# Fused cross-attention and ternary feed-forward on one core: the places of 22 weight tests, of two statistics and of the first weight transfers are changed

## The reference

```python
x = x + einsum(gelu_tanh(einsum(LN(x), ctx)) * einsum(LN(x), ctx), ctx)   # per batch, 120 context rows
h = silu(tlin(LN(x), w1)) * tlin(LN(x), w2)      # 256 -> 1024
h = gelu(tlin(h, h1))                            # 1024 -> 1024
h = gelu(tlin(h, h2))                            # 1024 -> 1024
x = x + tlin(h, w3)                              # 1024 -> 256
```

## Time and profile before

| what | value |
|---|---|
| median of three executions | 344.42 us (344.0 to 344.77) |
| the profiled execution's own time | 343.81 us |
| its span (first to last instruction) | 341.9 us |
| what lies around the span | 1.9 us |
| mean granted TensorE clock | 0.994 |
| busy: TensorE / VectorE / ScalarE / GpSimd | 325.9 / 265.4 / 219.1 / 47.2 us |
| HBM read, written | 49.36 MB, 6.29 MB |

### The profile page before, as it was taken

How to read it: one execution, slowest core, us unless ns; L and a number is a source line. 1 busy time by engine, 2 the same in 40 slices (tenths; PEclk the granted TensorE clock), 3 DMA queues, 4 the chain that set the end, 5 groups by cost and what they waited for, 6 DMA issues and landing times.

```text
span 341.9 us, 4758 instructions
## 1 busy us (share of the span) xinstructions
PE 325.9 (95%) x1636; PEld 273.7 (80%) x1636; DVE 265.4 (78%) x492; ACT 219.1 (64%) x367; POOL 47.2 (14%) x86
## 2 busy tenths in 40 slices
PE   7779999994999999999999999999999999999994
PEld 5579888883887888877999888888888888888894
DVE  3577887893898688988779857389798698987594
ACT  2345838545498584668973563687868588667850
POOL 6536021000000011300403001200001000010000
PEclk9999999998999999999999999999999999999999
DMA  5999997948464854765301521353553665333003
GB/s 162 292 276 314 207 280 248 404 143 269 156 215 149 281 196 175 231 209 176 123 2 20 226 75 59 142 195 137 195 186 123 230 255 194 123 123 125 0 11 121
DMA packets 23213, 60.22 MB, mean 176 GB/s; under 512 B 1680, under 2 KB 7184, under 8 KB 20880
## 3 DMA queue, kind: packets, MB, share of 16 engines
q0 software_dynamic: 13728, 37.75, 36.5%
q1 hardware_dynamic: 9456, 22.11, 18.9%
HBM read 49.36 MB, written 6.29 MB: 163 GB/s over the span
## 4 chain that ended last, share of the span: by engine, by line
PE 79%; DMA 7%; ACT 4%; DVE 4%; issue 3%; POOL 1%; SPq 0%; ACTq 0%; DVEq 0%; POOLq 0%
PE P L1280 53%; PE P L1232 15%; PE P L1309 7%; DMA xs<-in_x 3%; DMA W<-in_w 2%; DMA SLY<-in_w 2%; PE P L1188 2%; PE P L1204 2%; PE P L1196 1%; ACT TR L599 1%; DVE H L910 1%; ACT H L627 1%; ACT TR L593 1%; POOL W L442 1%; ACT SLY L533 0%
## 5 line engine op out<-in xcount | busy, mean ns | idle before, releaser
L1280 PE MATMUL P<-TR,WR 128*128 128x512 f32 x896 | 208.0, 393 | 5.0 <-ACT P L612 4.5
L1280 PEld LDWEIGHTS P<-TR,WR 128*128 128x128 f32 x896 | 168.5, 189 | 42.3 <-ACT P L612 5.0
L593 ACT ACTIVATE TR<-H 128x512 fp32r<-128x512 f32 x112 | 68.2, 625 | 29.5 <-DVE H L889 26.3
L894 DVE TENSOR_TENSOR TR<-H,TR 128x512 fp32r<-128x512 f32 x112 | 74.9, 687 | 13.3 <-ACT TR L593 10.8
L1232 PE MATMUL P<-X,W 128*128 128x512 f32 (+1 forms) x320 | 62.6, 351 | 0.1
L1232 PEld LDWEIGHTS P<-X,W 128*128 128x128 f32 x320 | 51.7, 189 | 8.1 <-DVE X L831 0.5
L889 DVE TENSOR_TENSOR H<-H 128x512 f32<-128x512 f32 x64 | 42.0, 683 | 0.0
L867 DVE SCALAR_TENSOR_TENSOR H<-P,sc,SLY 128x512 f32<-128x512 f32 (+1 forms) x40 | 25.2, 639 | 19.5 <-ACT SLY L583 10.0
L583 ACT ACTIVATE SLY<-P,sc 128x512 f32<-128x512 f32 (+1 forms) x40 | 23.8, 602 | 19.9 <-PE P L1232 17.5
L607 ACT ACTIVATE H<-P 128x512 f32<-128x512 f32 x48 | 27.8, 593 | 13.0 <-PE P L1280 13.0
L627 ACT ACTIVATE H<-H,sc 128x512 f32<-128x512 f32 x40 | 27.6, 719 | 12.5 <-DVE H L910 12.5
(11 more groups left out here) (70 smaller groups left out, 192.1 us busy)
## 6 DMA issues: line engine op xcount, KB each, us to landing
WR<-blocks_h POOLq DMA_DIRECT2D x16, 1024.0 KB, 4.6
WR<-in_h POOLq DMA_DIRECT2D x12, 1024.0 KB, 5.1
SLY<-in_h SPq DMA_DIRECT2D x9, 512.0 KB, 3.6
H<-in_h POOLq DMA_DIRECT2D x8, 512.0 KB, 12.2
blocks_h<-H SPq DMA_DIRECT2D x4, 1024.0 KB, 5.4
SLY<-in_w SPq DMA_DIRECT2D x6, 512.0 KB, 5.0
W<-in_w POOLq DMA_DIRECT2D x4, 512.0 KB, 6.2
WR<-in_w POOLq DMA_DIRECT2D x2, 1024.0 KB, 5.1
```

What stands on the lines that cost most here:

```text
L593: eng.activation(TR[:, f % RING, 0, :], operand(c, L, s, kk), ACT.Copy).then_inc(s_hi, 1)
L894: eng.tensor_tensor(TR[:, f % RING, 1, :], operand(c, L, s, kk), TR[:, f % RING, 0, :].bitcast(f32), ALU.subtract).then_inc(s_lo, 1)
L1280: out_ = eng.matmul(bank(c, L, s, m)[:, :], WR[r % WRING][:, at:at + 128], TR[:, f % RING, h, :], start=(s in FRESH[L] and kk == 0 and h = ...
```

## The change

- Test 0 no longer stands beside product (0, 0, 1): the first test is beside (0, 0, 2), and all later tests in pass 0 move by one place. The test beside `layer4` of pass 0 (`BESIDE4`) is gone. Pass 0 has nine tests in place of eleven (0 to 8).
- Pass 1 has thirteen: a third one in `layer1(3)` at m = 7, and two in place of one beside (1, 0, 6). Buffers, the waits of `load_check` and the waits for tests before buffers are reused follow the new numbers.
- GpSimd's order at the start: `rstd` of batch 1 ahead of `load_w(0,0,0)`, `rstd` of batch 2 and `load_w(0,0,5)` ahead of `load_raw(0)`.
- In `square`: for s = 4 and 5 VectorE makes four totals, then the test, then the four low parts. The statistics of batches 4, 5, 6 and 7 are spread over s = 2, 3, 4 and 6, and the two `scale` over s = 3 and 5.

```diff
--- before.py
+++ after.py
@@ -275,24 +275,23 @@
 
 
         TESTS = 22
-        BESIDE = {(0, 0, 1): (0,), (0, 0, 2): (1,), (0, 0, 6): (2, 3), (0, 1, 0): (4,), (0, 1, 1): (5,), (0, 1, 2): (6,),
-                  (0, 1, 4): (7,), (0, 1, 5): (8,), (0, 1, 6): (9,)}
-        BESIDE.update({(1, 0, 1): (13,), (1, 0, 2): (14,), (1, 0, 6): (15,)})
+        BESIDE = {(0, 0, 2): (0,), (0, 0, 6): (1, 2), (0, 1, 0): (3,), (0, 1, 1): (4,), (0, 1, 2): (5,),
+                  (0, 1, 4): (6,), (0, 1, 5): (7,), (0, 1, 6): (8,)}
+        BESIDE.update({(1, 0, 1): (12,), (1, 0, 2): (13,), (1, 0, 6): (14, 15)})
         BESIDE.update({(1, 1, p): (16 + p,) for p in range(6)})
-        BESIDE1 = {(3, 1): 11, (3, 2): 12}
-        BESIDE4 = {0: (10,), 1: ()}
+        BESIDE1 = {(3, 1): 9, (3, 2): 10, (3, 7): 11}
 
         def beside(c, L, s):
             return BESIDE.get((c, L, s), ())
 
         def tested(i):
 
-            if i < 11:
+            if i < 9:
                 n = 2 + i % 2
-            elif i < 15:
+            elif i < 13:
                 n = 1 - i % 2
             else:
-                n = (2, 3, 0, 1)[(i - 15) % 4]
+                n = (2, 3, 0, 1)[(i - 13) % 4]
             if n >= 2:
                 return (SL, Y)[n - 2].rearrange("p a t -> p (a t)")
             return (xn[0], xt)[n][:, :, :, :].rearrange("p a b d -> p (a b d)")
@@ -329,13 +328,13 @@
                 eng.dma_start(dst, raw(p)).then_inc(s_S[p], 16)
 
             def load_check(i):
-                if i in (0, 1, 15, 16):
+                if i in (0, 1, 13, 14):
 
                     eng.wait_ge(s_g, gate_no(1 if i < 2 else 3, 7) + 1)
-                elif i in (11, 12):
+                elif i in (9, 10):
 
                     eng.wait_ge(s_s, 8)
-                elif i < 15:
+                elif i < 13:
                     eng.wait_ge(s_fl, i - 1)
                 else:
                     eng.wait_ge(s_fl, i - 3)
@@ -374,13 +373,13 @@
             sums_out(2)
             sums_out(3)
             eng.dma_start(s3b[:, :], s3.broadcast_to([128, D])).then_inc(s_s3, 16)
-            for i in range(11):
+            for i in range(9):
                 load_check(i)
             for q in range(4):
                 eng.wait_ge(s_y2, q + 1)
                 b = (2, 3, 0, 1)[q]
                 eng.dma_start(out_v[b], xs[:, 2 * b:2 * b + 2, :]).then_inc(s_out, 16)
-            for i in range(11, TESTS):
+            for i in range(9, TESTS):
                 load_check(i)
             for q in range(2):
                 eng.wait_ge(s_y2, 4 + q + 1)
@@ -479,12 +478,13 @@
             rstd(0, 1, 1)
             rstd_half(1, 0)
             rstd_half(1, 1)
+            rstds(2, (1, 1))
             load_w(0, 0, 0)
+            rstds(3, (0, 2))
+            load_w(0, 0, 5)
             load_raw(0)
-            rstds(2, (1, 1), (0, 2))
-            load_w(0, 0, 5)
+            rstds(4, (0, 3))
             load_raw(1)
-            rstds(4, (0, 3))
             load_raw(2)
             load_raw(3)
             rstds(5, (1, 2), (1, 3))
@@ -578,7 +578,7 @@
                     eng.wait_ge(s_g, g - 1)
                 if (t, m) == (2, 0):
 
-                    eng.wait_ge(s_fl, 11)
+                    eng.wait_ge(s_fl, 9)
                 at = tokens1(t, p)
                 eng.activation(SL[:, g % 2, at], bank1(t, 2 * m, p)[:, at], ACT.Silu, scale=sc[:, m:m + 1]).then_inc(s_sl, 1)
 
@@ -737,8 +737,6 @@
                             copy_t(2 + i)
                         else:
                             gelu(c, 1, (1, 0), i)
-                for n in BESIDE4[c]:
-                    magnitude(n)
                 if c == 0:
                     gelu(0, 1, (1, 0), 2)
                     gelu(0, 1, (1, 0), 3)
@@ -930,10 +928,10 @@
             def square(c):
 
                 for s in range(NP):
-                    if s < 6:
+                    if s < 4:
                         for n in beside(c, 1, s):
                             test(n)
-                    if c == 0 and s in (4, 5):
+                    if c == 0 and s in (2, 3):
                         stats(0, 2 + s)
                     if s in (0, 1, 3):
                         add_up(c, 1, s + 1)
@@ -942,25 +940,30 @@
                             lo(c, 1, 3, i)
                         for i in range(4):
                             add(c, 1, 6, i)
+                    if c == 0 and s == 3:
+                        scale(0, 4)
                     if s in (4, 5):
+
                         for i in range(4):
                             total(c, 1, ((0, 1), (1, 1))[s - 4], i)
+                        for n in beside(c, 1, s):
+                            test(n)
+                        for i in range(4):
                             lo(c, 1, s + 1, i)
+                    if c == 0 and s == 4:
+                        stats(0, 6)
+                    if c == 0 and s == 5:
+                        scale(0, 5)
                     if s == 6:
                         for i in range(5):
                             if i < 4:
                                 total(c, 1, (0, 0), i)
                             if i >= 1:
                                 lo4(c, 1, i - 1)
-                    if c == 0 and s == 2:
-                        stats(0, 4)
-                        stats(0, 5)
-                    if c == 0 and s == 3:
-                        scale(0, 4)
-                        scale(0, 5)
-                    if s == 6:
                         for n in beside(c, 1, s):
                             test(n)
+                        if c == 0:
+                            stats(0, 7)
 
             def late_products(c):
 
@@ -1025,7 +1028,7 @@
                     eng.wait_ge(s_s3, 16)
                 if half == 1 and q == 0:
 
-                    eng.wait_ge(s_fl, (11, TESTS)[c])
+                    eng.wait_ge(s_fl, (9, TESTS)[c])
                 if q == 0:
                     eng.wait_ge(s_m4, 2 * c + (1 - half) + 1)
                 else:
@@ -1106,8 +1109,6 @@
                 square(c)
                 for k in range(4, 8):
                     lo4(c, 1, k)
-                for n in BESIDE4[c]:
-                    test(n)
                 if c == 0:
                     gate(4)
                     gate(5)
```

## The result

The changed kernel takes **333.59 us** at the median of four executions (333.28 to 333.92), the kernel before on the same chip 344.56 (344.0 to 344.77): a ratio of 0.9684, 95% interval 0.9667 to 0.9701. I had forecast 335.0 with a range from 333.8: faster, as forecast, but by 1.4 us more, and just outside the range. The profiled execution took 333.92 us with a span of 332.1 and a mean granted clock of 0.999.

What follows compares the result with a forecast made beforehand. TensorE was taken as the bound, busy 325.9 of 341.9 us. Gains of 1.48 (A), 7.45 (B and C) and 0.3 (D), 9.2 in all, took 343.81 to 334.6, put at 335.0 as a median; range 333.8 to 336.0.

Steps and rivals of the forecast that it cites:

- B: Pass 0, test 0 one product later: TensorE's 4.68 us wait and 1.47 us of lower clock go.
- C: Second square layer of pass 0, new order: weight loads' waits for totals go, about 1.3 us; 7.45 together with B.
- The stall: Product (0, 0, 1): test 0's Abs holds up the fourth put_back, so TensorE idles 4.68 us, then 1.47 lost to clock.
- rival 5: Pass 0: put_back waits for something other than the Abs; 342.9 us at best, near no change; chance 0.01.
- ScalarE reaches the Abs at its new place: Beside (0, 0, 2): ScalarE arrives at about 80.6, test 0's transfer lands at 80.8, so it waits 0.2 us.
- VectorE is late at product 4: Pass 0, totals of product 4: VectorE ready at 97.1, TensorE at 96.97; 0.2 us late, each us of later landing costs one.
- Part E: Pass 1, two tests more, in layer1(3) and beside (1, 0, 6): cost 0; without cover 1.1 us each.
- part A: The start: transfers issued behind rstd(1, 1) let batch 2 land in under 6.2 us; gain 1.48, ends 0 and 1.87.
- Rival 4: Slower: raw blocks for combine(0) land late, after over 25 us; at 27 us about 346 us; chance 0.02.
- The median is 0.6 above that execution: Whole kernel: the profiled execution's forecast of 334.6 us was raised to 335.0 for a median.
- part D: layer4 of pass 0, no test beside it: Abs and test leave the chain to weigh; gain 0.3 us, ends 0 and 0.4.
- The port rule: The start: load_w(0,0,0), issued just ahead of scale(1, 1), could hold it up on shared ports; start's gain 1.2, total 335.3.

Runs made afterwards that it cites:

- u_test0: The changed kernel with test 0 back beside product (0, 0, 1): 339.32 us, ratio 0.986.
- a_start: The kernel before with GpSimd's new order at the start alone: 341.81 us, ratio 0.9904.
- after_again: The changed kernel itself, run once more on another chip: 333.27 us, ratio 0.9674.
- after3: The changed kernel once more, beside three variants on one chip: 333.83 us, ratio 0.9696.
- the first four experiments: The kernel before with one edit each: GpSimd's start order, test 0's place, order of square(), test away from layer4; 341.81, 339.66, 341.89, 344.03 us.
- d_layer4: The kernel before with only the test beside layer4 of pass 0 moved to m = 7 of layer1(3): 344.03 us, ratio 0.9978.
- c_square: The kernel before with the new order in square() alone, old tests: 341.89 us, ratio 0.9909.
- a_half: The changed kernel with GpSimd's old start order, except that load_raw(0) goes behind the statistics of batches 2 and 3: 333.42 us, ratio 0.9672.

## Why the prediction was right and wrong

**Right.** The mechanism of the largest parts: B and C together gave 7.41 for 7.45. The stall is the Abs (`u_test0` brings back both it and the lower clock, `a_start` keeps both), so rival 5 is out. ScalarE reaches the Abs at its new place about when the transfer lands: it waited 0.32 us, forecast 0.2. VectorE is late at product 4, and each us of later landing costs one: `after_again` shows 0.76 us for a landing 0.74 later. Part E cost nothing (87.20 for 87.22). The condition of part A, a landing under 6.2 us, was met with room (2.6), since none of the 2 MB is ahead of batch 2 now, where I had counted on half. Rival 4's landing of over 25 us did come (the longest is 28.7), but not for the blocks of `combine(0)`: VectorE shows no wait near 41.

**Wrong, first: "The median is 0.6 above that execution".** Of that 0.6 I added 0.4 (335.0 for 334.6), carrying the distance of before's median from its profiled execution over to the changed kernel. It doesn't carry over. The changed kernel's median lies 0.33 below its profiled execution here, 1.35 below in `after_again` and 0.20 above in `after3`: which execution is profiled is chance. This step is 0.4 + 0.33 of the 1.4 us that I was off.

What the distance of before was made of is shown in part. The 16 executions of before on the chip of the first four experiments spread over 343.25 to 346.35 with a mean clock of 0.982 to 0.994, and I had read one of the fastest, at 0.994. The lower clock behind the stall costs 1.5 us in one execution and 2.4 in another (30 x 0.08, `a_start`), batch 2's late landing costs some 1.7 in four of the six traces with the old start, and in two of the six the clock fell near the start as well (1.3 us in `d_layer4`). None of the twelve traces with the new start has that fall, and none with test 0 moved has the stall, so both costs are smaller now. The spread is not gone: the changed kernel still spreads over 1.7 and 2.0 us on two chips, and its slowest execution, 335.0, has a mean clock of 1.0. Two candidates stand in traces, a late test 0 (0.76 in `after_again`) and the wait for a stored weight sum (0.55 in `after3`). Neither is as long as the spread, and the slowest execution on that chip was not profiled.

**Wrong, second: part D, "no more than some 0.4 in all".** Measured 0.96. I took the merged rows of the attention at their durations, as work, and counted only the bracketed waits; a merged row runs from first start to last end, gaps included, and the eight matmuls of one `turn`, for one, went from 1.35 to 1.04 us. Comparing whole stretches between anchors, as I did for the products, would have bounded it properly. And it is not D's: C alone gives 0.97 and D alone 0.74, as both make ScalarE and VectorE earlier for the same waits. This is 0.66 of the error.

**Wrong, third: part A, 1.48 for 1.71.** The gate that I took to be next, with a silu ending at 22.26, was the one with m = 5; m = 4 ran at 21.98 already, and `turn(1, 1)` came the full 1.76 earlier. The 0.23 more that A gave was offset by the -0.27 of the last stretch and the -0.04 of B and C, which is luck. I also took the late landing as a fixed property of the old order. It isn't: it was late in four traces of six, and at the median the old order costs 1.1 us on one chip and, across chips, 0.3 to 0.9 on another.

**The port rule.** GpSimd's issue ended at 22.26 and `scale(1, 1)` started at 22.35, with its usual 0.73, so the extra 0.3 that the prediction worked out for this case did not come: the two never met. The next pair, started at 23.50 with an issue under way from 23.32 to 24.12, took 1.03, as the pair of before did. The Trainium skill, SBUF — State Buffer, section Who interferes with whom, says that when VectorE works in a two-port mode, whoever issues first has the shared ports for the whole instruction and the other is fully blocked. The rows agree in so far as the pair is longer beside an issue, by 0.3 us, which is less than the 0.62 that was left of the issue. No run separates the issue from other causes of the 0.3.

**Still open.** `a_start` alone gains 3.0 us at the median (2.2 to 4.4 by its interval) and `c_square` alone 2.9, where their traces show 1.7 and 2.0. The rest would have to be less clock loss in typical executions, and the runs don't separate that from chance. What decides whether batch 2 lands late under the old order wasn't tested beyond the order of the issues given above, and the spread of the changed kernel has no shown cause.

## What to carry to other kernels

A wait of TensorE of several us can cost more than its length. Behind this one it ran at the lower clock, for an amount that differs between executions. So price a stall from several executions, and don't carry the distance between a median and one profiled execution over to a changed kernel. When a transfer waits for its turn, read its own landing time and not only the wait of its reader: an engine that came late enough sees no wait. Compare whole stretches between fixed anchors, as merged rows hide gaps. When two edits feed the same late chain, expect them not to add. Put optional work where the engine that does it waits for the bound engine.

## What the runs showed of the hardware

- A 256 KB transfer issued by SyncE 0.3 to 1.2 us behind 512 KB of weights on GpSimd's queue, with 2 MB of them in all, landed after 5.0 to 8.0 us in six traces; issued 2.4 us behind 1 MB, after 3.6 (`a_half`, one trace); with none of these ahead, after 2.5 to 2.7 in eleven.
- Behind a wait of TensorE of 4.5 to 4.7 us the granted clock averaged 0.95 in one trace and 0.92 in another over some 30 us. Near the start it was 0.57 over 4 us in `c_square`, behind an idle time of 1.16 us after which it did not fall in the other traces. Whole executions of before lay between 0.982 and 0.995.
- Stores of 1 MB landed in 5.4 us at the median before and in 9.8 after, with 512 KB loads issued 10 us later; the loads went from 12.2 to 14.5, the longest from 16.2 to 28.7. In one of three traces of the changed kernel TensorE waited 0.35 us for a stored sum.
